# TensorE waits four times per piece instead of ten in the expert loop of a spiking-attention and mixture-of-experts block

## The reference

```
x = x + conv(_ln_c(x), ...)        # spiking attention, 4 x 32 x 49 tokens of 128 channels
t = tokens of x                    # 6272 tokens
t = t + ffn(_ln_t(t), Wg, W1, b1, W2, b2)

def ffn(x, Wg, W1, b1, W2, b2):    # E = 8 experts, K = 2 per token, hidden width 512
    gate = softmax(xt @ Wg)
    topv, topi = top_k(gate, 2);  topv = topv / (sum(topv) + 1e-6)
    scores = zeros((T, E)).at[..., topi].set(topv)
    for e in range(E):
        h = gelu(xt @ W1[e] + b1[e], approximate=False)
        ye = h @ W2[e] + b2[e]
        out = out + ye * scores[:, e:e + 1]
```

## Time and profile before

| what | value |
|---|---|
| time, median of 3 runs | 534.23 us (533.28 to 534.72) |
| profiled execution: span from first to last instruction | 531.9 us |
| difference of the two (outside the span, or another execution) | 2.3 us |
| DVE busy | 384.5 us (72%) |
| ACT busy | 305.1 us (57%) |
| POOL busy | 222.5 us (42%) |
| DMA queues moved | 43.05 MB |

### The profile page before, as it was taken

How to read it: one execution, slowest core, us unless ns; L and a number is a source line. 1 busy time by engine, 2 the same in 40 slices (tenths; PEclk the granted TensorE clock), 3 DMA queues, 4 the chain that set the end, 5 groups by cost and what they waited for, 6 DMA issues and landing times.

```text
span 531.9 us, 10740 instructions
## 1 busy us (share of the span) xinstructions
PE 346.8 (65%) x2516; PEld 287.3 (54%) x2516; DVE 384.5 (72%) x1368; ACT 305.1 (57%) x709; POOL 222.5 (42%) x233
## 2 busy tenths in 40 slices
PE   2466565657742758354410699999999999999200
PEld 1233233435421435242310599999999999999200
DVE  4699999998898798979770466666666666666186
ACT  3458684766647556362310477766666676776073
POOL 3000000027173037375777055666656566665400
PEclk9977777775576775655555699999999999999755
DMA  6901001102121011221542222222222222221299
GB/s 176 287 8 25 16 15 22 17 18 67 25 67 47 9 36 59 48 67 43 194 136 81 61 76 76 75 63 78 68 75 66 69 75 70 75 62 50 74 352 311
DMA packets 62123, 43.05 MB, mean 81 GB/s; under 512 B 29057, under 2 KB 56745, under 8 KB 62096
## 3 DMA queue, kind: packets, MB, share of 16 engines
q1 hardware_dynamic: 53648, 28.85, 20.5%
q0 software_dynamic: 6720, 12.97, 7.7%
q10 hardware_dynamic: 1728, 0.94, 0.7%
HBM read 22.09 MB, written 19.91 MB: 79 GB/s over the span
## 4 chain that ended last, share of the span: by engine, by line
PE 48%; DVE 35%; issue 5%; ACT 4%; POOL 3%; DMA 3%; ACTq 1%; POOLq 0%; SPq 0%; DVEq 0%
PE PS L1177 19%; DVE U L897 6%; PE PS L1167 6%; DVE VV L889 5%; DVE H_all L879 5%; PE PS L1169 5%; PE PS L1168 5%; PE PS L1110 3%; PE PS L1047 3%; POOL by_expert L427 3%; DVE stats L647 2%; PE PS L1154 2%; DVE X L1011 2%; PE PS L1038 2%; DVE spikes L907 1%
## 5 line engine op out<-in xcount | busy, mean ns | idle before, releaser
L427 POOL DMA_INDIRECT by_expert<-XG,place x98 | 97.9, 999 | 188.2 <-DVE place L801 159.9
L443 POOL DMA_INDIRECT by_token<-osp,target x112 | 119.8, 1069 | 88.5 <-DVE osp L981 55.5
L1177 PE MATMUL PS<-w_now,hid 128*128 128x128 f32 x896 | 108.8, 275 | 0.0
L1177 PEld LDWEIGHTS PS<-w_now,hid 128*128 128x128 f32 x896 | 104.8, 192 | 0.0
L577 ACT ACTIVATE hid<-PS,b1c 128x256 f32<-128x256 f32 x224 | 87.9, 480 | 5.3 <-PE PS L1169 3.1
L1167 PE MATMUL PS<-rows_high,w_high 128*128 128x256 f32 x224 | 68.5, 306 | 1.0 <-DVE rows_low L965 0.3
L583 ACT ACTIVATE w_now<-W_s 128x512 f32 x56 | 35.6, 635 | 53.6 <-PE PS L1177 44.7
L1169 PE MATMUL PS<-rows_high,w_low 128*128 128x256 f32 x224 | 63.7, 284 | 0.0
L1168 PE MATMUL PS<-rows_low,w_high 128*128 128x256 f32 x224 | 63.6, 284 | 0.0
L1047 PE MATMUL PS<-xT,wT 128*128 128x392 f32 x96 | 57.1, 722 | 0.7 <-ACT xT L488 0.7
L959 DVE CAST w_high<-H_all 128x512 fp32r x56 | 24.1, 430 | 39.4 <-PE PS L1169 38.1
(11 more groups left out here) (156 smaller groups left out, 590.4 us busy)
## 6 DMA issues: line engine op xcount, KB each, us to landing
rows_in<-by_expert SPq DMA_DIRECT2D x56, 130.0 KB, 2.1
X<-in_x SPq DMA_DIRECT2D x7, 448.0 KB, 6.1
out<-X SPq DMA_DIRECT2D x7, 448.0 KB, 5.7
xT<-by_token SPq DMA_DIRECT2D x3, 896.0 KB, 7.3
H_all<-in_L_ffn_W SPq DMA_DIRECT2D x1, 2048.0 KB, 9.7
by_token<-osp,target POOLq DMA_INDIRECT x112
H_all<-by_token SPq DMA_DIRECT2D x2, 896.0 KB, 11.4
W_s<-by_token SPq DMA_DIRECT2D x2, 896.0 KB, 11.7
```

Of the source, the lines that this page charges most:

```text
L427: pool.indirect_dma_start(by_expert, bass.IndirectOffsetOnAxis(ap=place[g % SENDING][:, k, r:r + 1], axis=0), XG[g % SENDING][:, r, :], No ...
L443: pool.indirect_dma_start(by_token, bass.IndirectOffsetOnAxis(ap=target[b][:, a:a + 1], axis=0), rows_out[b][:, a, :], None, bounds_check= ...
L1177: m = pe.matmul(PS[:, 4 + b % 2, a * 128:a * 128 + 128], hid[b % 2][:, hb, a * 128:a * 128 + 128], w2_now[b % 2][:, hb * C:hb * C + C], st ...
```

## The change

Of the ten waits per piece (one in `turn_piece`, six in `up`, three in `down`) four are left. In `up` of piece j the wait for `w1_set` goes; the four waits for `gelu_done`, one ahead of each hidden block, each for one more GELU of piece j-1, become one wait ahead of the first block, for `4 * j`, which is all four GELUs of piece j-1. In `down` the waits for `w2_set` and for `gelu_done` go, except for the last piece, which keeps the one for `gelu_done`. All other engines' programs stay as they are, and so do all products.

```diff
             def up(j, b, after_first=True):
-                pe.wait_ge(w1_set, 2 * j + 2)
+
                 pe.wait_ge(piece_copied, 2 * j + 2)
+                if after_first:
+                    pe.wait_ge(gelu_done, HB * j)
                 for hb in range(HB):
-                    if after_first:
-                        pe.wait_ge(gelu_done, HB * (j - 1) + hb + 1)
...
-            def down(j, b):
-                pe.wait_ge(w2_set, j + 1)
+            def down(j, b, last=False):
+
+                if last:
+                    pe.wait_ge(gelu_done, HB * (j + 1))
                 pe.wait_ge(rows_ready, j + 1)
-                pe.wait_ge(gelu_done, HB * (j + 1))
...
             down(PIECES - 2, DEEP - 2)
-            down(PIECES - 1, DEEP - 1)
+            down(PIECES - 1, DEEP - 1, last=True)
```

## The result

The changed kernel takes 541.42 us (median of 4 runs, 540.11 to 542.20) against 534.48 us of the kernel before (4 runs). The ratio is 1.0141, 95% interval 1.0107 to 1.0175: it is slower by 6.9 us. The forecast was slower, 542.4 us, with a range of 540.6 to 545.1. The profiled execution has a span of 539.3 us, 7.4 more than before.

The account below looks back on a forecast made before the run. TensorE's own program was taken to set the pace in the expert loop. Delays of 11.9 us, less 3.6 for hidden holes and 0 for dropped waits, give +8.2 on 534.2: 542.4 us, range 540.6 to 545.1.

Parts of the forecast that it names:

- The one wait is no wait that another one stands for: At ups of pieces 4i+1, the merged wait delays the start until the fourth GELU ends, typically from 357.06 to 357.96.
- pause: TensorE idle some 0.9 us ahead of each of 13 ups of pieces 4i+1, waiting for the fourth GELU.
- Its size: Delay at 13 ups: 1.10 first, 1.04 second, 0.885 at eleven others, 11.9 us in all.
- The holes are hidden: Eleven 0.30 us TensorE idles ahead of ups, from late VectorE, vanish behind the delays: 0.33 us each, -3.6 us.
- The waits left out are worth nothing: Dropping the w1_set wait in the up and two waits ahead of the down gains 0, steps hidden under products.
- The upper end of 4.0 us: Most the dropped waits could return, if the up's slower product starts (0.118 against 0.112 us) were due to waits.
- The sum: Whole kernel: 11.9 - 3.6 - 0 = +8.2 us (+1.5%), giving 542.4 us; chance 0.83.
- The 2.3 us added to the span: Part outside the program's instructions, by which the profiled span lies under the median; taken as untouched by the change.
- A: Rival: pauses are paid but VectorE's holes ahead of ups are not hidden; +10.7, 544.9 us; chance 0.06.
- B: Rival: pauses cost TensorE its high clock; 576 us if one piece per pass, 545.0 if a single one; chance 0.06.
- C: Rival: dropped waits do pace TensorE, two exposed per piece at 0.11 us, 12.3 us back; 530.1 us; chance 0.03.
- D: Rival: GELU's semaphore rises before its record ends, so the one wait costs nothing; -1.2 us, 533.0 us; chance 0.02.

Follow-up runs that it names:

- e2: Kernel before with only the four GELU waits merged into one ahead of the first block, other waits kept: 541.85 us, ratio to before 1.0135.
- e1: Changed kernel with the four GELU waits, one per hidden block, put back and the other dropped waits still out: 532.69 us, ratio to before 0.9958.
- e9: Changed kernel with ScalarE's loop turned by half a piece, so its branch stands behind the GELUs: 534.87 us, ratio to before 1.0014.
- e15: Kernel before with only the w1_set wait left out of the up: 533.21 us, ratio to before 0.9987.
- e12: Kernel before, ten waits kept, with VectorE's loop turned so its branch stands where it waits for a down anyway: 531.10 us, ratio to before 0.9932.
- e13: Changed kernel with only VectorE's loop turned: 542.55 us, ratio to the kernel before 1.0177.
- e4: Changed kernel with ScalarE's loop made 2 passes of 26 pieces instead of 13 of 4: 537.01 us, ratio to the kernel before 1.0040.
- e14: Kernel before with only the w1_set wait left out of the up; its single run took 1106.93 us.

## Why the prediction was right

- *The one wait is no wait that another one stands for.* Right: e2 is the whole loss, e1 has none of it. Each pause is where it was predicted, ahead of the up of a piece 4i+1, ends 0.05 us behind the fourth GELU, and twelve of the 13 go when their table loads go (e9; the first keeps its load and its pause).
- *Its size.* Predicted 11.9 us, measured as the excess over the usual step: 1.09 at the first, 1.03 at the second, 4.28 - 3.43 = 0.85 at the other eleven, 11.5 together. The term was 0.035 us too large at each of the eleven. From W2's copy to the fourth GELU's end I read 357.91 - 353.83 = 4.08 us in the trace of before (where that copy starts at 353.83); in the changed kernel it is 360.56 - 356.53 = 4.03. The start of the table load has moved by 0.06 against the copy (1.22 to 1.16). e15, with the holes only 0.11 us shorter, and e12, with ten waits and no holes, have the 4.03 as well, so only the kernel before, with its full holes, shows the longer time; by what path is open.
- *The holes are hidden.* Right, -3.6 us: each step of 3.77 is 3.43 now, and e13 shows that removing their cause changes nothing any more.
- *The waits left out are worth nothing.* Right for this kernel. Where the holes are still open the one for `w1_set` is worth 11 x 0.11 = 1.2 us (e15; 0.9 in the length of its loop), as the prediction had it for a shorter path. The upper end of 4.0 us, for waits between the up's products, is refuted by the changed kernel, which has none there: its blocks come 0.34 us apart (360.61, 360.95), 0.35 before, and its steps still take 3.43.
- *The sum.* +8.2 predicted; +7.8 in the loop, +7.4 in the span (the loop started 0.4 us earlier in this execution), +6.9 in the medians, whose interval reaches from +5.7 to +9.4. The pauses, 0.4 too large, are the term that was mis-sized; that the medians moved by 0.9 less than the loop lies within their interval. The 2.3 us added to the span for the part outside the program were too much: the profiled execution of the changed kernel took 541.09 with a span of 539.3, 1.8 apart, and the other runs on record lie 1.7 to 2.2 above their spans, so a part of the 2.3, some 0.5, came from comparing different executions.
- *Rivals.* A (the holes stay) is refuted by the eleven steps of 3.43 and by e13. B (the clock) did not come about: the granted clock is 1.00 from 301.5 to 502.8. The Trainium skill ("TensorE: Matmul & The Clock Gate", section "A second HAM failure mode: psum-queue depth-cycling") tells of another kernel, in which short idle times between groups of matmuls made the clock swing. This trace shows no such swing at twelve pauses of 0.8 to 1.0 us, one in four pieces. The prediction's argument against B, that 3.7 idle us had passed at the end before the level fell, was weaker than it looked: in e4 a pause of 3.04 us came just ahead of a fall. C (the waits pace PE) is refuted by the steps of 3.43 and by e2, which keeps three more waits and has the same loop; D (no cost) by e2 and by the 0.05 us at all 13 pauses.
- *A reading that was off.* The prediction has PE's slices at 9 "for the last 300 us but the tail". A slice is 13.3 us, and the 14 slices at 9 are some 190 us, from about 306 us on the earlier trace rows. Nothing in the sum hangs on it.

## What to carry to other kernels

A wait may be dropped when another one implies it, and moved only if the work it waits for is done by the new place at every pass: merging four staggered waits into one moves the last of them forward, and the price is paid where the producer is at its latest, which here was one piece in four behind a loop branch and a table load. Look in the trace for the end of each producer beside the start of its consumer before calling a wait redundant; waits that are met in time cost nothing that shows here, so there was little to win. A loop's branch and what the compiler puts behind it belong where the engine would wait anyway: turning VectorE's loop by a few instructions brought more (3.2 us of the loop) than leaving out waits did (1.0 us, e1).

## What the runs showed of the hardware that was not expected

- With the GELUs ahead of the loop and at the end of each pass, ScalarE's loop holds no table load: 1 of 1.283 us in place of 13 (e9).
- A branch back over 26 pieces of ScalarE's code took 2.4 to 2.5 us longer than one over 4 (from the start of W2's copy to that of the table load 3.62 against 1.16 to 1.22 us), at the one such branch that e4 takes. Why was not measured.
- TensorE kept its high clock over twelve pauses of 0.8 to 1.0 us in 200 us, and went to the low level for some 3.4 us after a pause of 3.04 us, 1.0 us behind its end (e4).
- In one execution TensorE was 3.5 times slower throughout the expert loop (loads 0.42 us apart, not 0.12) with the granted clock recorded as 1.00 (e14).
